# Moving GpSimd's normalised row behind the folding of the maxima, and score blocks ahead of its users

## What is computed

```python
x = x + attn(layernorm(x))       # qkv = x @ w_attn; 16 heads of 8, causal softmax; y @ w_proj
x = x + ffn(layernorm(x))
# ffn(x):
xn = rmsnorm(x, gamma)
q = (xn @ wq.T)                                   # 2 x 8 heads x 64
sim = einsum("pbnhd,hkpd->pbnhk", q, keys)        # 32 scores for each of the two halves
sx, ix = top_k(sim[0], 16); sy, iy = top_k(sim[1], 16)
scores, pk = top_k(sx[..., :, None] + sy[..., None, :], 16)   # 16 best of the pairs
indices = ix * 32 + iy at pk
h = einsum("bnd,bnhkd->bnhk", xn, table_down[indices])
h = gelu(h) * softmax(scores)
out = einsum("bnhk,bnhkd->bnd", h, table_up[indices])
```

## Time and profile before

| what | value |
|---|---|
| median of 3 runs | 846.98 us (845.35 to 848.09) |
| the profiled execution, whole | 848.22 us |
| its span, first to last instruction | 846.4 us |
| mean granted clock of TensorE | 0.970 of full |
| PE, DVE, ACT, POOL busy, share of the span | 83%, 89%, 80%, 78% |
| a repeat of the same fold instruction in the loop | 383.34 to 431.04 us, 47.70 us |

### The profile page before, as it was taken

One profiled execution on the slowest core, in us unless ns is written; L12 is line 12 of the kernel. 1 busy time (PEld: TensorE's weight loads), 2 busy tenths in 40 slices (PEclk: granted clock), 3 DMA queues, 4 the chain that ended last, 5 costly groups with the idle time before them and its releaser, 6 DMA issues.

```text
span 846.4 us, 20984 instructions
## 1 busy us (share of the span) xinstructions
PE 699.7 (83%) x6127; PEld 487.9 (58%) x6192; DVE 755.6 (89%) x2936; ACT 676.2 (80%) x927; POOL 658.4 (78%) x370
## 2 busy tenths in 40 slices
PE   3886878897979888897979888897979888887766
PEld 2652546574646656574646656574646656564646
DVE  4419699999999999999999999999999999898986
ACT  1364788989888898989888898988888898878671
POOL 2111488898979799897979799897979799787862
PEclk9898989999999999999999999999999999898998
DMA  5412121120303121120302121120303121010000
GB/s 143 90 41 56 21 55 28 32 55 10 74 2 67 19 60 26 31 56 10 73 3 67 20 60 26 28 58 10 73 3 67 20 49 34 1 33 1 21 6 7
DMA packets 34736, 32.53 MB, mean 38 GB/s; under 512 B 5520, under 2 KB 32784, under 8 KB 32976
## 3 DMA queue, kind: packets, MB, share of 16 engines
q1 hardware_dynamic: 34608, 32.12, 17.1%
q10 hardware_dynamic: 96, 0.02, 0.0%
HBM read 19.93 MB, written 5.24 MB: 30 GB/s over the span
## 4 chain that ended last, share of the span: by engine, by line
PE 46%; DVE 27%; issue 14%; ACT 9%; POOL 1%; ACTq 1%; another core or an unknown queue 1%; DVEq 1%; DMA 0%; POOLq 0%
DVE prob L1069 13%; PE misc L1313 6%; PE misc L1473 6%; PE score L1350 5%; PE score L1293 5%; PE score L1402 5%; PE score L1263 4%; PE score L1295 3%; ACT prob L752 3%; PE misc L1315 3%; ACT late_scores L618 2%; DVE late_scores L915 2%; DVE halves L909 2%; ACT probs L645 2%; PE score L1266 2%
## 5 line engine op out<-in xcount | busy, mean ns | idle before, releaser
L518 POOL TENSOR_TENSOR acc<-acc,prob 128x1024 f32<-128x1024 f32 x184 | 435.4, 2367 | 16.2 <-POOL acc L518 0.6
L1069 DVE SCALAR_TENSOR_TENSOR prob<-score,cut,prob 128x1024 f32<-128x1024 f32 x256 | 314.2, 1277 | 17.6 <-ACT prob L752 16.2
L752 ACT ACTIVATE prob<-score,neg_lse 128x1024 f32<-128x1024 f32 x256 | 278.8, 1118 | 33.2 <-PE score L1402 25.1
L1402 PE MATMUL score<-sel_unit,pieces_t 128*128 128x512 bf16 x480 | 148.8, 395 | 73.1 <-DVE prob L1069 48.7
L645 ACT ACTIVATE probs<-score 128x512 f32<-128x512 f32 x192 | 109.9, 596 | 27.2 <-PE score L1295 23.2
L518 POOL TENSOR_TENSOR acc<-prob 128x1024 f32<-128x1024 f32 x32 | 75.6, 2363 | 63.9 <-DVE prob L1069 63.9
L1402 PEld LDWEIGHTS score<-sel_unit,pieces_t 128*128 128x128 f16 x512 | 39.8, 101 | 121.1 <-DVE prob L1069 86.6
L1350 PEld LDWEIGHTS score<-xn_kept,wdt 128*128 128x128 f32 x480 | 72.4, 191 | 29.4 <-issue 6.4
L1350 PE MATMUL score<-xn_kept,wdt 128*128 128x128 f32 x480 | 84.9, 278 | 3.8 <-DVE prob L1069 3.4
L1263 PE MATMUL score<-k_ahead,q_ahead 128*128 128x256 bf16 (+1 forms) x512 | 70.3, 246 | 10.7 <-ACT probs L645 6.7
L1473 PEld LDWEIGHTS misc<-wu,gated_t 128*128 128x128 f32 x480 | 66.4, 200 | 9.7 <-issue 1.4
(11 more groups left out here) (150 smaller groups left out, 1433.8 us busy)
## 6 DMA issues: line engine op xcount, KB each, us to landing
q_scratch<-qk_piece SPq DMA_DIRECT2D x16, 192.0 KB, 2.1
q_ahead<-q_scratch SPq DMA_DIRECT2D x16, 192.0 KB
q_stack<-q_scratch SPq DMA_DIRECT2D x16, 192.0 KB
xin<-x SPq DMA_DIRECT2D x16, 128.0 KB, 3.0
q_ahead<-q_scratch SPq DMA_DIRECT2D x16, 128.0 KB
q_stack<-q_scratch SPq DMA_DIRECT2D x16, 128.0 KB
xres<-x SPq DMA_DIRECT2D x16, 128.0 KB, 3.3
x_kept<-x SPq DMA_DIRECT2D x16, 128.0 KB, 2.0
```

The source lines that it names most:

```text
L518: eng.tensor_tensor(acc[:, j, :], so_far, prob[:, j * FH + h, :], ALU.add).then_inc(acc_added, FH - h if last else 1)
L752: eng.activation(prob[:, g, :], score[g % BUFS][:, :], ACT.Exp, bias=neg_lse[:, j, h:h + 1]).then_inc(prob_made, 1)
L1069: eng.scalar_tensor_tensor(prob[:, g, :], score[g % BUFS][:, :], cut[:, j, h:h + 1], prob[:, g, :], ALU.is_ge, ALU.mult).then_inc(prob_mas ...
L1402: ins = eng.matmul(score[g % BUFS][:, cols], pieces_t[:, j, h, :], sel_unit[:, cols], start=True, stop=True)
```

## The change

- GpSimd's `make_xhat(i + 3)` waits, from tile 3 on, until `fold_max(i + 2)` is done.
- On PE, blocks 3 and 4 stand ahead of the transposes of xhat, and block 5 ahead of `project_qkv`. Two and two matmuls of `keep_busy` around block 7 become four behind it, together with the wait for `v_next`.
- On ACT, the exponentials of blocks 3 and 4 stand ahead of `xhat_back`, and each of the row's later steps stands one exponential later than before.
- On DVE, `qk_remainder` stands behind the mask of block 6; it stood behind that of block 4.
- At the end, PE takes one block more (`sum_last_tile(3)`), DVE adds three late blocks and no longer four, and `keep_busy` with 8 and with 4 matmuls stands around the last sum.

```diff
 def make_xhat(b):                                   # gpsimd
+    if later(b - 2 if isinstance(b, int) else b):
+        eng.wait_ge(max_step, every(max_step, b - 1))
     eng.wait_ge(ln1_step, every(ln1_step, b))
...
 # scalar, iteration
+                if f:
+                    pair_probs(i, 0, 3)
+                    pair_probs(i, 0, 4)
                 if p:
                     xhat_back(i + 3)
                 if m:
                     copy_v(i + 2)
                 if f:
-                    pair_probs(i, 0, 3)
+                    pair_probs(i, 0, 5)
                 if a:
                     sim_high_piece(i + 1, 0)
                 if f:
-                    pair_probs(i, 0, 4)
+                    pair_probs(i, 0, 6)
                 if p:
                     qk_high_piece(i + 3)
                     v_back(i + 3)
                 if f:
-                    pair_probs(i, 0, 5)
+                    pair_probs(i, 0, 7)
                 if a:
                     sim_high_piece(i + 1, 1)
                 if f:
-                    pair_probs(i, 0, 6)
+                    pair_probs(i, 1, 0)
                 if p:
                     qk_middle_piece(i + 3)
...
 # vector, iteration
                     mask(i, 0, 4)
+                    mask(i, 0, 5)
+                    mask(i, 0, 6)
                 if p:
                     qk_remainder(i + 3)
                 if f:
-                    mask(i, 0, 5)
-                    mask(i, 0, 6)
                     mask(i, 0, 7)
...
 # tensor, finish_last
-                eng.wait_ge(late_added, 4)
-                sum_transposed(misc, prob[:, 2 * FH - 5, :], False, True, acc_tp)
+                keep_busy(score[2], 8)
+                eng.wait_ge(late_added, 3)
+                sum_transposed(misc, prob[:, 2 * FH - 4, :], False, True, acc_tp)
+                keep_busy(score[2], 4)
...
 # tensor, iteration
+                if f:
+                    pair_scores(i, 0, 3, a, m)
+                    if a:
+                        pair_scores(i, 0, 4, a, m)
                 if p:
                     xhat_transpose(i + 3, sim_kept, at(sim_kept, i + 1, 1))
-                if f:
-                    pair_scores(i, 0, 3, a, m)
+                if f and a:
+                    pair_scores(i, 0, 5, a, m)
                 if p:
                     project_qkv(i + 3, sim_kept, i + 1)
                 if f:
-                    for n in range(4, 7):
+                    for n in range(6 if a else 4, 7):
                         pair_scores(i, 0, n, a, m)
...
-                if p:
-                    eng.wait_ge(v_next_made, every(v_next_made, i + 3))
-                    keep_busy(misc[0], 2)
                 if f:
                     pair_scores(i, 0, 7, a, m)
...
                 if p:
-                    keep_busy(misc[0], 2)
+                    eng.wait_ge(v_next_made, every(v_next_made, i + 3))
+                    keep_busy(misc[0], 4)
...
                 if f and not a:
                     sum_last_tile(2)
+                    sum_last_tile(3)
                     finish_last()
```

More of the change, by code:

```diff
@@ L268, in build @@
         acc_added = signal("acc_added", TILES * (FH - 1))
-        late_added = signal("late_added", 4)
+        late_added = signal("late_added", 3)
         last_hidden = signal("last_hidden", 2)
@@ L859, in iteration @@
                 if f:
-                    pair_probs(i, 0, 6)
+                    pair_probs(i, 1, 0)
                 if p:
                     qk_middle_piece(i + 3)
-                if f:
-                    pair_probs(i, 0, 7)
                 if m:
@@ L867, in iteration @@
                 if f:
-                    for h in range(FH):
+                    for h in range(1, FH):
                         pair_probs(i, 1, h)
-                        if d and h == (5 if a else 0):
+                        if d and h == (5 if a else 1):
                             fin_back(i - 1)
@@ L1074, in add_late_heads @@
                 eng.wait_ge(prob_masked, at(prob_masked, LAST, TILES * FH))
-                for n in range(4):
+                for n in range(3):
                     g = 2 * FH - 2 - n
```

## The result

The changed kernel takes 858.72 us (median of 4 runs, 858.32 to 863.39), the one before in the same comparison 847.46 (4 runs, 845.35 to 848.09). The ratio is 1.0141, with a 95% interval of 1.0117 to 1.0164: **slower by 1.4%, 11.3 us**. The profiled execution took 858.84 with a span of 857.1, against 848.22 and 846.4: 10.7 us more. One of the four executions of the changed kernel, that of 863.39, had a mean granted clock of 0.966 where the other three have 0.978 to 0.980; it has no trace, and what follows is read from that of 858.84.

A forecast was written before the change was run, and what follows sets the result against it. It took PE from block 8 to block 12 as the bound. Per iteration 0.62 gained, 1.29 lost: +8.0 us in twelve; with -0.4, 0 and -1.8 outside, +5.8 on 846.98 gives 852.8, range 845 to 857.

The forecast's parts named there:

- The fold: First fold instruction to first mask: moving make_xhat behind the fold gives DVE 0.62 us an iteration.
- GpSimd behind the fold: GpSimd's three make_xhat instructions run beside the first masks, end near 2.2 us after the first, and cost nothing.
- The walk: Seven-step chain from block 4 to expert_output, which starts at 9.72 for 8.43 after the first mask: 1.29 us lost.
- Steps 1 and 2: Block 4 ends 3.12 us after the first mask; xhat_back, behind its exponential, runs from 4.24 to 4.62.
- Step 3: project_qkv on PE starts at 4.68 us after the first mask and lasts 1.23, to 5.91.
- GpSimd's low piece: It waits for the middle piece, so GpSimd's sums end about 0.2 us later against mask 14: costed at nothing.
- Outside the loop: Iteration 0 gives -0.4 us, iterations 13 and 14 give 0 within 0.3 each way, and the kernel's end -1.8.
- The end: With three late additions and no pause on PE, the output product starts 1.8 us sooner; bounds -1.3 and -3.3.
- No net change: Rival: mask 6 isn't made to wait, expert_output starts at 9.09, eating the fold's 0.62; 845.3 to 849 us, chance 0.15.
- the faster case: Rival: expert_output has slack and starts before 9.05, so DVE loses its waits; 828.7 to 844 us, chance 0.11.
- The falling clock: Rival: longer PE idle time drops TensorE's clock to 1.2 GHz once an iteration; 865 to 871 us, chance 0.04.
- The fold was freed: Negates a rival: another GpSimd instruction slides into the fold, so nothing is gained there; 860.3 us, chance 0.03.

The follow-up runs named there:

- wait only: The kernel before with only GpSimd's new wait in make_xhat added, every order as it was: 865.74 us against 847.37, ratio 1.0210.
- both of these: The changed kernel with GpSimd's low piece one sum later and block 6 ahead of project_qkv on PE: 842.88 us against 845.91, ratio 0.9961.
- the fillers back: The changed kernel with two keep_busy matmuls ahead of and two behind block 7 again, and the v_next wait with them: 873.15 us against 845.91.

## Why the prediction was wrong in size

It said slower, in the main for the right reasons, and 852.8 where 858.7 was measured. By its own steps:

**The fold.** Forecast 0.62 gained, measured 0.68. Right.

**GpSimd behind the fold.** Its three instructions end 396.29 + 0.61 - 394.53 = 2.37 after the first mask, forecast 2.2, and the masks beside them keep their step of 1.19. Right.

**The walk.** Steps 1 and 2 hold within 0.02: `xhat_back` forecast at 4.24, measured 398.79 - 394.53 = 4.26. Step 3 forecast the start at 4.68 (measured 4.68) and a length of 1.23 from the earlier trace rows, and the projection took 1.34, since the earlier trace rows shows it behind a block and here it stands behind a wait. Mask 6 so starts at 7.87 and not 7.77, the remainder at 9.07 and not 8.96, and `expert_output` at 9.80 and not 9.72. From there to block 12 it forecast 5.30 as before; it took 5.41 (block 12 at 409.74), again with a first group behind a wait (1.16 where the earlier trace rows has 1.05). These two are what the stretch was missed by, +1.49 for +1.29: twelve times 0.2, 2.4 us.

**GpSimd's low piece.** This is the step that failed: "its sums end about 0.2 us later against mask 14 than before. I cost this at nothing: PE takes the sums only when it has come to them." They end 0.4 later, and PE isn't the one who pays. The wait for the middle piece was forecast at 1 to 1.5 us and is 1.88. (The middle piece stood behind exponential 6 before, so it moved by two exponentials; the list of the change, which says one, is wrong there.) All of the wait goes on to GpSimd's last row, and the masks, later by 1.49, hide the most of it. `sim_low` stands behind the sums on GpSimd and shuts out DVE's small instruction. The cost is 0.39 an iteration, 4.7 us in twelve, and the prediction had it at nothing. The low piece moved by one sum gives it back, with the 0.24 that the kernel before had paid.

**The loop.** 12 x (0.39 + 1.49 - 0.68) = 14.4 for 8.0.

**Outside the loop.** For iteration 0 it took -0.4. Its mask stretch shrank by 0.96 (22.57 to 21.61), but what follows grew by 1.37, together +0.41. The 1.37 has the same cause as the loop's 0.39: DVE's small instruction takes 0.69 for 0.17 and ends with the first piece of `sim_low`, and the next one takes 1.07 for 0.16 and ends with the second. With the low piece later both are short again, and tile 0 to 1 takes 49.37 in place of 50.59. Iterations 13 and 14 were costed at 0 within 0.3, and together gave 2.3 us, 1.75 of it in tile 13. The shifted ACT copies aren't needed for that: *wait only*, with the old order there, has 43.36 us too, where the kernel before has 45.48 and the changed one 43.73. What differs is the clock: in tile 13 it stood at the lower level for 9.2 us before, for 6.7 in the changed kernel and for 3.4 in *wait only*. It can't be this amount alone: *both of these* had it low for 6.8 us there and took 43.26. The kernel before is the one with a fall 9.2 us after the first mask of that tile, and its masks take 21.98, those of the changed kernel 19.84. That the clock is the cause was not tested; it stays open. The end was forecast at -1.8 and gave -2.25; alone it gave -1.85.

**The sum.** +14.4 in the loop; outside +0.41 (tile 0) - 1.75 - 0.57 - 2.25 = -4.2; with the prologue's +0.39 that is the +10.6 of the traces. Forecast were +8.0 and -2.2. So the loop was missed by 6.4 us, and the gains outside, 2.0 more than forecast and in part by an open cause, brought the total nearer to the forecast than its working was: that is luck.

**The rivals.** No net change and the faster case needed `expert_output` at 9.09 and 9.05 or sooner, and it stood at 9.80. The falling clock wasn't the cause in the traced execution of the changed kernel (1.00 over the loop), though five of the nine other kernels had it in their loops. The fold was freed. The range reached to 857.0 and ended below the result, because the low piece had a single value, nothing, and no bound on its other side.

## What to carry over

When an instruction is made to wait, follow its engine's queue to the end, and ask not only who waits for its results but what else then runs beside which engine: here 0.4 us of lateness on GpSimd, with slack towards every reader, came back as 0.4 us on DVE. Take the duration of a group from a row in which it stands as it will stand, behind a wait or behind other work. Of a chain that crosses four engines, moving its first links one place sooner (837.1 us) was worth more than moving the block that it delays (842.9).

## What the runs showed of the hardware

- A DVE instruction over 128 x 2 numbers takes 0.17 us alone and, beside a GpSimd instruction that is under way, up to 0.86 in the changed kernel's loop and 0.98 in *the fillers back*; it ends within 0.03 us of that one. The next, a `TENSOR_TENSOR` over as few, takes 0.16 or 1.07 in the same way.
- The first fp32 matmuls behind a wait cost PE 0.11 us more than the same ones behind other matmuls (0.70 against 0.59, and 1.16 against 1.05; for the whole projection from start to start 1.34 against 1.23). The bf16 score blocks show 0.01 to 0.02 (0.61 against 0.59). The Trainium skill ("TensorE: Matmul & The Clock Gate", section "Single matmul latency") has a lone bf16 matmul at full clock take 398 cycles more than its columns; at 2.4 GHz that is an estimate of 0.17 us by that page. The measured 0.11 and 0.02 are less, and they decide here.
- TensorE's clock fell inside the loop in some iterations and not in others of one kernel, with the same instructions and the same idle times ahead of the fall. A fall cost an iteration 0.3 to 2.6 us (52.17 for 49.61 at most, with the clock at the lower level for 10.2 us). Matmuls put into the longest gap removed the falls there, and others came six us later in the iteration.
